# Mask products in front of the value products, and the statistics of the input rows behind the row maxima, in a fused attention and expert layer

## The reference

```
shift = silu(t) @ W_ada.T + b_ada
h     = ln(x, ln1_g, ln1_b) + shift
qkv   = (h @ Wqkv.T).reshape(b, n, 3, 16, 64)
q, k  = ln over the 64 features of a head, each with its own gain and bias
attn  = softmax(q k^T / 8)           # 16 heads, 256 x 256 scores each
x     = x + (attn v) @ Wout.T
gate  = softmax(x @ Wgate.T)          # 8 experts
each expert takes the 512 tokens with its highest gates:
  y = gelu(ln(token) @ fc1.T + b1) @ fc2.T + b2, times the gate, added to the token
```

## Time and profile before

| | |
|---|---|
| median of three runs | 1202.66 us |
| profiled execution: its own time | 1205.0 us |
| span of its instructions | 1203.2 us |
| PE busy | 1088.6 us, 90% of the span, 8291 products |
| DVE busy | 801.8 us, 67% |
| ACT busy | 774.7 us, 64% |
| POOL busy | 571.3 us, 47% |
| mean granted PE clock | 0.956 of full speed |

### The profile page before, as it was taken

The page is one execution under the profiler, slowest core; times in us unless marked ns, Lnnn a source line. Parts: engine busy times, 40 slices in busy tenths (PEclk is TensorE's granted clock), DMA queues, the critical chain, the costliest instruction groups (busy, mean ns, idle before and its releaser), DMA issues.

```text
span 1203.2 us, 24526 instructions
## 1 busy us (share of the span) xinstructions
PE 1088.6 (90%) x8291; PEld 839.1 (70%) x8291; DVE 801.8 (67%) x1602; ACT 774.7 (64%) x1454; POOL 571.3 (47%) x614
## 2 busy tenths in 40 slices
PE   4699999999999999999999999999994136999996
PEld 3467777777777777777777777777763035988995
DVE  7556757676666767576667667576655794777773
ACT  4476868787786878787786878787772104445541
POOL 2465646454554546454554646454561003455332
PEclk9899999999999999999999999999998557999998
DMA  5000010000001010000001010000003203455322
GB/s 174 18 1 28 1 36 19 17 17 17 17 17 35 0 35 17 17 17 17 17 17 35 0 35 17 17 9 19 10 18 139 69 15 110 119 171 134 105 25 29
DMA packets 32285, 48.60 MB, mean 40 GB/s; under 512 B 7920, under 2 KB 28528, under 8 KB 30960
## 3 DMA queue, kind: packets, MB, share of 16 engines
q1 hardware_dynamic: 26096, 39.49, 10.1%
q0 software_dynamic: 6144, 8.52, 3.9%
HBM read 35.29 MB, written 12.71 MB: 40 GB/s over the span
## 4 chain that ended last, share of the span: by engine, by line
PE 85%; DVE 7%; POOL 3%; issue 2%; ACT 2%; DMA 1%; SPq 0%; DVEq 0%; POOLq 0%; ACTq 0%
PE ch L481 14%; PE ch L483 12%; PE ch L482 12%; PE av L1365 10%; PE sc L1390 9%; PE sc L1381 5%; PE pq L1343 5%; PE av L1369 5%; PE mx L1401 2%; DVE hit L733 2%; PE sc L481 1%; PE sc L482 1%; PE sc L483 1%; PE ch L1415 1%; PE ch L1328 1%
## 5 line engine op out<-in xcount | busy, mean ns | idle before, releaser
L962 POOL TENSOR_TENSOR qk_lo<-qkT,qk_hi 128x512 fp32r<-128x512 f32 x128 | 170.1, 1329 | 254.5 <-ACT qk_hi L1041 231.6
L957 POOL TENSOR_TENSOR prob_sum<-prob 128x512 f32<-128x512 f32 x128 | 165.5, 1293 | 78.5 <-ACT prob L1061 78.5
L1220 DVE TENSOR_TENSOR av<-av,rec 128x256 f32<-128x256 f32 x128 | 55.2, 431 | 211.0 <-ACT rec L1057 211.0
L481 PE MATMUL ch<-w_hi,hT_lo 128*128 128x512 f32 x384 | 172.7, 450 | 7.3 <-DVE w_lo L1123 7.3
L1061 ACT ACTIVATE prob<-sc 128x1024 f32<-128x1024 f32 x128 | 131.0, 1024 | 40.0 <-PE sc L1390 38.2
L1239 DVE TENSOR_REDUCE m<-mx 128x4 bf16<-128x1024 f32 x128 | 155.5, 1215 | 0.8 <-PE mx L1401 0.8
L482 PE MATMUL ch<-w_lo,hT_hi 128*128 128x512 f32 x384 | 153.5, 400 | 0.0
L483 PE MATMUL ch<-w_hi,hT_hi 128*128 128x512 f32 x384 | 153.3, 399 | 0.0
L860 DVE TENSOR_TENSOR qn<-raw,rstd 128x512 f32<-128x512 f32 x128 | 122.0, 1010 | 36.2 <-POOL rstd L924 36.2
L1365 PE MATMUL av<-prob,V 128*64 128x256 f32 x1024 | 138.8, 392 | 2.1 <-ACT prob L1061 2.1
L967 POOL TENSOR_TENSOR o_lo<-oT,o_hi 128x256 fp32r<-128x256 f32 x128 | 100.9, 789 | 26.2 <-ACT o_hi L1066 26.2
(11 more groups left out here) (202 smaller groups left out, 2789.4 us busy)
## 6 DMA issues: line engine op xcount, KB each, us to landing
fcw<-experts SPq DMA_DIRECT2D x8, 2048.0 KB, 9.0
x_sb<-x SPq DMA_DIRECT2D x16, 256.0 KB, 2.7
xr_sb<-x SPq DMA_DIRECT2D x16, 256.0 KB, 2.7
out<-tok SPq DMA_DIRECT2D x16, 256.0 KB, 2.2
rows_dram<-xh SPq DMA_DIRECT2D x16, 256.0 KB, 2.2
prob<-w_qkvT SPq DMA_DIRECT2D x2, 512.0 KB, 7.9
qn<-w_qkvT SPq DMA_DIRECT2D x2, 512.0 KB, 8.6
V<-w_qkvT SPq DMA_DIRECT2D x2, 512.0 KB, 8.1
```

The lines of the kernel that those rows point to most:

```text
L481: nc.tensor.matmul(psum, l_lo, r_hi, start=first, stop=False)
L957: nc.gpsimd.tensor_tensor(prob_sum[(hp - 1) % 2][:, :, :], pr[:, :, 0, :], pr[:, :, 1, :], ALU.add).then_inc(prob_summed, 1)
L962: nc.gpsimd.tensor_tensor(qk_lo[par][:, :], qkT[par][:, :], qk_hi[par][:, :].bitcast(F32), ALU.subtract).then_inc(lo_ready, 1)
```

## The change

On PE the mask products of a step stand ahead of the value products of the pair before, in every step but 3, where they stay behind them. Their two waits move with them. On DVE the statistics of the input rows in step 3 go from a place ahead of the first sum of squares to one behind the maxima. No instruction is added or taken away.

```diff
@@ DVE, batch()
-                    if hp == 3 and has_second(b):
-                        need(x_in, (b + 3) * 16)
-                        row_stats(x_sb, 0)
                     if hp in (0, 3, 4, 7) and (cur if hp < 2 else nxt):
                         head_sums(b, hp, 0)
...
                         nc.vector.tensor_reduce(m[(hp + 1) % 2][:, :], mx[:, :].rearrange("p (a j) -> p a j", a=4),
                                                 AX.X, ALU.max).then_inc(max_ready, 1)
+                    if hp == 3 and has_second(b):
+                        need(x_in, (b + 3) * 16)
+                        row_stats(x_sb, 0)
@@ PE
+            def mask(u, par):
+
+                need(prob_ready, u)
+                need(max_ready, u + 1)
+                for hh in range(2):
+                    both = sc[:, hh * TT * N:(hh + 1) * TT * N].rearrange("p (j i n) -> p j i n", j=TT, i=TT)
+                    for it in range(TT):
+                        nc.tensor.matmul(both[:, :, it, :], m[par][:, hh * TT + it:hh * TT + it + 1].to_broadcast([P, P]),
+                                         neg_ident[:, :].rearrange("p (o n) -> p o n", o=1).to_broadcast([P, TT, P]),
+                                         start=(it == 0), stop=False)
@@ PE, batch()
+                    if cur and hp != 3:
+                        mask(u, hp % 2)
                     if (cur and hp > 0) or (hp == 0 and prv):
 
                         need(prob_ready, u)
...
                     if cur:
 
-                        need(prob_ready, u)
-                        need(max_ready, u + 1)
+                        if hp == 3:
+                            mask(u, hp % 2)
                         need(lo_ready, u + 1)
                         par = hp % 2
-                        for hh in range(2):
-                            both = sc[:, hh * TT * N:(hh + 1) * TT * N].rearrange("p (j i n) -> p j i n", j=TT, i=TT)
-                            for it in range(TT):
-                                nc.tensor.matmul(both[:, :, it, :], m[par][:, hh * TT + it:hh * TT + it + 1].to_broadcast([P, P]),
-                                                 neg_ident[:, :].rearrange("p (o n) -> p o n", o=1).to_broadcast([P, TT, P]),
-                                                 start=(it == 0), stop=False)
```

## The result

The change makes the kernel slower. Nine runs of the changed kernel have a median of 1206.57 us (1203.38 to 1209.84), beside 1202.66 (1200.98 to 1204.65) for nine of before on the same chip: ratio 1.0027, 95% interval 1.0014 to 1.004, so +3.2 us (1.7 to 4.8), less than half a per cent but clear of no change. A second set of five runs on another chip gives 1.0038 (1.0024 to 1.0051). The forecast was 1201.5, with a range that ended at 1206. The profiled execution took 1207.02, its span 1205.2.

What follows compares the result with a forecast made beforehand. PE was taken as the bound, always busy in middle batches. Fourteen batches gaining 0.29 us (-4.1) and the last batch's +2.9 gave -1.2 on 1205.0, or 1201.5 at the runs' median; range 1196.5 to 1206.

Steps and rivals of the forecast that it cites:

- The change of form: PE, each step with the mask moved: one array form change falls away, gaining 0.09 us, 0.63 a batch.
- The rival in which the change of precision eats the gain: Chunk to mask on PE takes 0.33, no step gains, last batch loses +2.9 to +3.5; 1205.9 us; chance 0.10.
- The signal: From the end of the maxima on DVE to PE's mask products: taken as 0.05 us.
- that of step 6: PE's wait for the maxima in step 6 of a middle batch: nothing, but with no reserve.
- Step 4 and the statistics: Step 4: with statistics moved behind the maxima, their 1.15 us are hidden and PE waits only 0.06.
- Step 7 and the lock: Step 7: DVE and POOL exclude each other, swallowing the normalisations' late start; PE waits 0.28 for the maxima.
- The delay: Maxima of step 7: a 0.24 delay could go through, making PE's wait 0.52 and the time 1204.9; chance 0.10.
- The fast rival (no wait in step 7): PE doesn't wait for maxima in step 7, a middle batch gains 0.57; 1197.6 us; chance 0.17.
- The circle of the last batch: Last batch, steps 4 to 7: attended, logarithm, division, maxima, mask, values, sums take 5.54 a step, not 4.70; +2.9 us.
- Batch 0: The first batch: its change in time was counted at nothing.
- The prediction's rival in which the mask fills PE's wait for `prob_sum`: Last batch: mask products fill PE's wait between values and sums, five steps gain 0.54 each; 1195.9 us; chance 0.08.

Runs made afterwards that it cites:

- Experiment 3: Changed kernel with the mask's two waits in the other order, the maxima's wait carried by the first weight load; 1203.65 us, ratio 0.9996 to the kernel before.
- experiment 4: Changed kernel with the mask moved but the statistics left in front of the maxima; 1221.07 us, ratio 1.0147 to the kernel before.
- experiment 10: Changed kernel, mask's waits swapped, old mask order in step 7 of all batches and in the last batch from step 2; 1195.35 us, ratio 0.9939 to before.
- experiment 6: Changed kernel plus products with discarded results ahead of the mask in steps 4 to 7 of the last batch; 1204.18 us, ratio 1.0003 to before.
- Experiments 1: Changed kernel with the mask back behind the value products in the last batch from step 2 on; 1200.86 us, ratio 0.9976 to before.
- experiment 2: Kernel before with the mask in front only in steps 2 and 4 to 7 of the last batch, statistics not moved; 1207.99 us, ratio 1.0037.
- filler: The kernel of experiment 6, the changed one plus discarded products in the last batch; 1204.18 us, and 1205.11 us when run again.

## Why the prediction was wrong

**The change of form: right.** 0.09 a step was taken; a middle batch shows it in steps 0, 1 and 5, where nothing waits (-0.09, -0.11, -0.10), and 0.24 from chunk to mask. The rival in which the change of precision eats the gain is out.

**The signal: the term that was mis-sized in every batch.** This step of the prediction failed. It was read as 0.05 from the exponentials, whose wait the value products carry. For the maxima it is 0.15, by the order of two waits (0.06 with the order turned). So the wait in step 4 is 0.14 instead of 0.06 and that of step 6, counted at nothing "but with no reserve", 0.08; with them a middle batch gains 0.13 instead of 0.29, and batches 1 to 14 give -2.4 instead of -4.1. Experiment 3 puts 0.14 of the missing 0.16 back. In step 7 the 0.20 lost (0.19 forecast) hides the error: the masks of steps 6 and 7 both follow the maxima, so their distance is that of the maxima, 6.23 in after and 6.22 swapped, whatever a signal takes.

**Step 4 and the statistics: right.** Without the second edit step 4 loses 1.21 (experiment 4), with it 0.05 by the signal above.

**Step 7 and the lock: right.** The delay was not passed on: normalisations 3.90 instead of 4.12, step 7 +0.20 and not +0.43. This agrees with the lock; no run here tests the lock by itself. The fast rival (no wait in step 7) didn't come either; it comes only when step 7 keeps its old order (experiment 10).

**The circle of the last batch: right in kind, 0.6 too small.** Forecast +2.9; +3.48 at full clock (experiment 6). Steps 4 to 7 lose 0.67, 1.01, 0.49 and 1.10, together 3.27: the masks stand 5.58 to 5.67 apart (the clock's 1.32 taken off the 6.90), not 5.54, and swapped waits take 0.35 off the batch. Step 2 loses 0.43; it was to lose 0.18. The prediction's own terms also sum to 22.16 - 18.81 - 0.54 = 2.81, where rounding gave 2.9. Experiments 1 and 2 place the whole loss of this batch there.

**The clock: missing.** In the last batch the prediction had no term for it, and gave no reason for leaving it out. It cost 1.32 us in one trace and 1.33 in another, by the difference to filler, some 0.65 in the traces of experiments 2 and 4, and nothing in that of experiment 3, where PE is idle as much (3.28 us busy of 885 to 890). That filling PE's idle time keeps it up is shown by two pairs of traces; what decides where it falls, or whether, stays open.

**Batch 0: counted at nothing, about -0.2.** The net is small, but its parts are not. The prediction's rival in which the mask fills PE's wait for `prob_sum` was set at the last batch, and it did not come there; it came in step 1 of batch 0, where that wait is over 4 us long (-0.97).

The sum: -4.1 + 2.9 = -1.2 was forecast. With the signal -2.4 + 3.5, batch 0 -0.2 and the clock 1.3 it is +2.2. The two measured ratios give +3.2 (1.7 to 4.8) and +4.6 (2.9 to 6.1). The two recorded executions differ by 2.0 (1207.0 and 1205.0), but the one of before lies 2.3 above its kernel's median and the one of after only 0.5 above. The 1.0 to 2.4 us between the sum and the measured differences I can't place: the first scores of batch 0 came between 43.9 and 46.3 us in the traces of all kernels, enough to cover it, and no experiment here holds the start still.

## What to carry to other kernels

Before a wait is asked for earlier, work out its reserve in every step and at the end of the loop, where the cover that hides it in the middle is missing; waits of 1.1 to 1.8 us in four steps of one batch outweighed the 2.4 us that fourteen batches had gained, and changing only the steps with reserve (with the waits in the right order) turned +0.3% into -0.6%. Where an instruction waits for two signals, put the one that comes last so that it isn't the extra one, and measure the signal on the wait that will really be the late one. New idle time on PE can have a second price, the clock behind it.

## What the runs showed of the hardware that was not expected

- Two waits ahead of one product are not alike: a signal reached the product after 0.05 to 0.06 us where its wait came first in the code, and after 0.14 to 0.15 where it came second. Over the kernel that is some 2.4 us by the traces.
- The granted clock fell to 0.83 over 10 us (0.66 in the worst stretch of 5, experiment 2) after idle times of 1.5 and 1.8 us in steps of 5.6 us, although PE had work for 3.53 us of 885 to 890. Waits about as long left it at 1.00 in the trace of experiment 3. With some 1.6 us of spare products a step (1.1 us in step 6) it stayed at 1.00 in both traces.
- A bf16 product behind an fp32 one of the same form starts after 0.24 us; a change of form costs 0.09 to 0.10 more.
